# Graph layers with pre-norms on one core: the variance of an older group ahead of the tick's head on VectorE, its logarithm and exponential ahead of the tick's first activations on ScalarE

## The reference, cut

```python
h = jnp.maximum(_layernorm(x, axis=-1), 0.0)
x = x + _L0_gnn_ref(h, edge_attr_32, src, dst, ...)   # attention over the edges, segment sums
h = jnp.maximum(_layernorm(x, axis=-1), 0.0)
x = x + _L1_gnn_ref(h, src, dst, ...)                 # one linear layer, mean by degrees
h = jnp.maximum(_layernorm(x, axis=-1), 0.0)
x = x + _L2_gnn_ref(h, edge_index, ...)               # two graph convolutions, with loops
h = jnp.maximum(_layernorm(x, axis=-1), 0.0)
x = x + _L3_gnn_ref(h, edge_index, ...)               # two graph convolutions, with loops
...
def _layernorm(x, axis=-1, eps=1e-05):
    m = jnp.mean(x, axis=axis, keepdims=True)
    v = jnp.var(x, axis=axis, keepdims=True)
    return (x - m) / jnp.sqrt(v + eps)
```

## Time and profile before

| | before |
|---|---|
| median of 3 runs | 2837.82 us (2832.29 to 2838.57) |
| the profiled execution's own time | 2831.61 us |
| its span | 2829.6 us |
| TensorE busy | 1862.6 us (66%) |
| VectorE busy | 1963.3 us (69%) |
| ScalarE busy | 1101.4 us (39%) |
| GpSimd busy | 1862.3 us (66%) |

### The profile page before, as it was taken

How to read it: one execution, slowest core, us unless ns; L and a number is a source line. 1 busy time by engine, 2 the same in 40 slices (tenths; PEclk the granted TensorE clock), 3 DMA queues, 4 the chain that set the end, 5 groups by cost and what they waited for, 6 DMA issues and landing times.

```text
span 2829.6 us, 25622 instructions
## 1 busy us (share of the span) xinstructions
PE 1862.6 (66%) x6464; PEld 875.8 (31%) x6464; DVE 1963.3 (69%) x3488; ACT 1101.4 (39%) x2157; POOL 1862.3 (66%) x1775
## 2 busy tenths in 40 slices
PE   1688778761888567777588856677488868882000
PEld 0333333320344233332244423333244434431000
DVE  4777777743777658999699959999599959972000
ACT  0112121120566435444366625555366636650000
POOL 0777777765775075552677756564577757777776
PEclk7889898975899879999799979999799979995555
DMA  0222222221455434332344434444334434442000
GB/s 15 57 64 64 64 77 64 64 63 44 146 176 176 158 100 136 107 109 95 89 120 128 120 90 146 153 146 149 104 121 125 123 101 140 144 131 63 23 21 20
DMA packets 228924, 285.58 MB, mean 101 GB/s; under 512 B 85309, under 2 KB 100697, under 8 KB 228652
## 3 DMA queue, kind: packets, MB, share of 16 engines
q1 hardware_dynamic: 172332, 257.60, 28.7%
q0 software_dynamic: 56448, 26.34, 5.2%
HBM read 173.01 MB, written 136.00 MB: 109 GB/s over the span
## 4 chain that ended last, share of the span: by engine, by line
DVE 28%; PE 16%; issue 13%; POOL 11%; ACT 6%; DMA 1%; DVEq 0%; SPq 0%; ACTq 0%; POOLq 0%
POOL out_dram L1705 7%; PE bank L1004 6%; DVE mn_total L1400 5%; DVE node_h L1208 5%; POOL mn_ring L447 4%; DVE node_h L1253 2%; PE bank L1756 2%; ACT node_square L1129 2%; DVE node_x L1232 2%; DVE mn_mean L1422 2%; DVE mn_cent L1424 2%; DVE mn_h L1480 2%; PE bank L1008 2%; PE bank L1013 2%; PE bank L998 2%
## 5 line engine op out<-in xcount | busy, mean ns | idle before, releaser
L447 POOL DMA_INDIRECT mn_ring<-slot_rows,addr_i x980 | 1042.4, 1064 | 620.6 <-issue 286.1
L1004 PE MATMUL bank<-node_x,center 128*128 128x512 f32 x492 | 258.4, 640 | 101.9 <-DVE node_h L1208 97.7
L447 POOL DMA_INDIRECT fr_xin<-in_x_dram,src_i x196 | 210.2, 1073 | 125.2 <-issue 125.2
L1008 PE MATMUL bank<-node_square,mean 128*128 128x512 f32 x492 | 263.3, 618 | 35.9 <-ACT node_std L1108 35.9
L447 POOL DMA_INDIRECT found<-node_table,look_i x196 | 210.7, 1075 | 89.1 <-issue 69.1
L1013 PE MATMUL bank<-node_h,wconv 128*128 128x512 f32 x492 | 267.0, 626 | 0.0
L447 POOL DMA_INDIRECT fr_xin<-in_x_dram,dst_i x196 | 204.2, 1042 | 59.7 <-issue 59.7
L595 PE MATMUL bank<-fr_s_lo,fr_s_hi 128*128 128x392 f16 x392 | 149.2, 381 | 138.0 <-DVE fr_d_lo L714 136.7
L1705 POOL DMA_INDIRECT out_dram<-keep,scat_i x196 | 192.6, 983 | 62.4 <-issue 62.4
L1018 PE MATMUL bank<-node_act,wconv 128*128 128x512 f32 x442 | 232.3, 608 | 1.2 <-ACT node_act L1123 1.2
L1123 ACT ACTIVATE node_act<-bank,bias 128x512 f32<-128x512 f32 x246 | 167.9, 682 | 126.1 <-PE bank L1013 125.8
(11 more groups left out here) (320 smaller groups left out, 3857.2 us busy)
## 6 DMA issues: line engine op xcount, KB each, us to landing
mn_ring<-local SPq DMA_DIRECT2D x120, 256.0 KB, 4.3
node_x_in<-in_x_dram SPq DMA_DIRECT2D x98, 256.0 KB, 3.0
out_dram<-node_rows SPq DMA_DIRECT2D x98, 256.0 KB, 3.3
mn_rin<-res SPq DMA_DIRECT2D x96, 256.0 KB, 3.3
local<-node_rows SPq DMA_DIRECT2D x96, 256.0 KB, 2.5
slot_rows<-keep SPq DMA_DIRECT2D x96, 256.0 KB, 2.0
mn_fcol<-f_rows SPq DMA_DIRECT2D x192, 128.0 KB, 4.1
res<-mn_x SPq DMA_DIRECT2D x72, 256.0 KB, 2.5
```

Source lines behind the costliest of these rows:

```text
L447: return eng.indirect_dma_start(out=dest, out_offset=None, in_=table, in_offset=bass.IndirectOffsetOnAxis(ap=index, axis=0), bounds_check= ...
L1004: pe.matmul(bank[i][:, :], C["center"][:, :], src, start=True, stop=True).then_inc(s["centered"][i], 1)
L1008: pe.matmul(bank[4][:, :], C["mean"][:, :], nd.square[:, i - 1, :], start=True, stop=True) \
```

## The change

Two calls change their places. On VectorE `variance` of the older group goes ahead of the tick's `head`; on ScalarE `deviation` of the older group goes ahead of the tick's `begin`. Nothing is added or taken away, no wait is changed, and the last group of a stage and all iterations without a tick keep their order.

```diff
--- before.py
+++ after.py
@@ -1548,10 +1548,11 @@
                         finish(st, g - 1)
                     if g < n - 1:
                         gather_sum(st, g + 1)
+                    if st in NORMS and g > 0:
+                        variance(st, g - 1)
                     for t in ticks[i][:1]:
                         head(t)
                     if st in NORMS and g > 0:
-                        variance(st, g - 1)
                         normalise(st, g - 1)
                     if g == n - 1:
                         finish(st, g)
@@ -1841,10 +1842,9 @@
                 for i, (st, g) in enumerate(order):
                     if st in NORMS and g > 0:
                         squares(norm_at(st, g - 1), g - 1)
+                        deviation(norm_at(st, g - 1), g - 1)
                     for t in ticks[i][:1]:
                         begin(t)
-                    if st in NORMS and g > 0:
-                        deviation(norm_at(st, g - 1), g - 1)
                     if st != "A":
                         mix(i, st, g)
                     for t in ticks[i]:
```

## The result

| | before | after |
|---|---|---|
| median of 4 runs each, taken together | 2835.07 us (2832.29 to 2838.57) | 2851.03 us (2848.83 to 2854.07) |
| the profiled execution's own time | 2831.61 us | 2848.83 us |
| its span | 2829.6 us | 2846.9 us |
| TensorE busy | 1862.6 us (66%) | 1871.2 us (66%) |
| VectorE busy | 1963.3 us (69%) | 1971.0 us (69%) |

The account below looks back on a forecast made before the run. A chain around several engines, none full, was taken to bound each norm-stage iteration. Stage A +10.2, B +0.5 and D +10.9 made +21.6 on 2831.6: 2853, or 2859 us on the runs' median scale; range 2844 to 2878.

Parts of the forecast that it names:

- both roads to L1208: Stage A: delay through ScalarE's last exponential, or through TensorE's L1008 and L1018 to L1232; both give +0.69 us.
- the 18 iterations of the forecast: Stage A: fifteen steady periods and three like them, each 0.69 us longer, 12.4 us in all.
- The three in which ScalarE waits inside the tick: Stage A: iterations where ScalarE waits for TensorE and the early pair helps: -1.1, -0.8 and -0.4 us.
- the half of the forecast: Stages B and D: longer gaps before L1008 make the clock fall in every second iteration, none certain.
- the 0.61: Stages B and D: VectorE's 0.61 us wait before mn_h goes; B keeps 0.52 an iteration, D nothing.
- the rival in which it falls nearly every time: Stages B and D: clock falls nearly always; +36 us, 2874, or +55, 2892 at 1.97 each in D; chance 0.14.
- +0.95: Stage D: cost in us of one clock fall, L1008 and L1018 both slow; 18 x 0.5 x 0.95 = 8.6.
- D's first iteration: Stage D: variance behind a gather, the tick's activations now after it, TensorE resuming at low clock; 2.3 us.
- The rival of the held clock: Stages B and D: the clock never falls; B -5.6, D +2.3, A +10.2: +7 us, 2845; chance 0.13.
- The rule that half of all time at the lower clock is lost: Stages B and D: as a rival, half of each 6.8 us fall lost, sixteen times 3.4: +69, 2907; chance 0.03.
- the cancelling one: Stage A: unseen slack takes half of the 0.69 us while the clock holds: +1, 2838; chance 0.06.
- The rival of a faster kernel: All norm stages: mn_h's wait binds everywhere; B and D give 18.7 us, A about 0.3 x 20: 2813; chance 0.04.

Follow-up runs that it names:

- e3: The changed kernel with ScalarE's old order restored in stage A alone, so the change acts in B and D: 2846.3 us, ratio 1.0038 to before.
- e6: The kernel before with the change's ScalarE order in stage A alone, B and D as before, on a second chip: ratio 1.0006 to before.
- e2: The kernel before with only ScalarE's small logarithm and exponential moved ahead, VectorE's order as before: 2909.27 us, ratio 1.0255.
- e4: The changed kernel with matmul L1013 done three times instead of once in ticks from the 30th on, shortening TensorE's gap before L1008: 2947.29 us, ratio 1.0397 to before.
- e8: The changed kernel once more, unaltered, on a second chip where before took 3326.86 us: ratio 1.0039 to before.
- e1: The kernel before with only the variance on VectorE moved ahead, ScalarE's order as before: 2816.8 us, ratio 0.9943.
- e5: VectorE as in the changed kernel, ScalarE's small pair between the tick's rectifier and logarithm, on a second chip: ratio 0.9933 to before.
- e12: The changed kernel again, unaltered, on a third chip where before took 3374.26 us: ratio 1.0039 to before.

## Why the prediction was right, and where it was off

- **Stage A: right in mechanism and in the period, its total partly by luck.** The wait came to stand before the work of the tick: 0.75 us idle before L1827 where about 0.75 was said, the period 12.69 for a forecast of 12.66, both roads to L1208 as described. e3 and e6 show it from both sides. Of the 18 iterations of the forecast 17 cost 0.72 and the one from 736.1 cost 0.54, together 12.7 for 12.4. The three in which ScalarE waits inside the tick (from 712.6, 722.9 and 943.8) gave -2.25, -0.55 and -0.21, -3.0 for the -2.3 forecast. So the profiled stage came out at +9.74 for +10.2. The same orders cost +12.9 in e2 and e4, where the clock fell in an early iteration; the forecast had no term for that.
- **Stage B: the mechanism right, the sum by errors that cancel.** The period is 14.92 where the clock holds, 0.52 under 15.44. A fall costs back 0.52, so most long iterations are at 15.44, where 15.8 was forecast. L1008 waits 2.24, forecast 2.2, in nine of the last eleven iterations with a head, and three of these nine are long, fewer than the half of the forecast. The eleven bring -4.0 (about -0.9 by the forecast), the six heads ahead of them scatter from -1.4 to +1.5 and bring +1.6 (about -1.1 by the forecast): -2.3 for -2.0. The first iteration, which like the second has no head, costs 0.5 for 2.0, the second 0.6 for 0.5. Why the first costs so little no run shows.
- **Stage D, what is kept: right.** Nothing of the 0.61, 14.96 for 14.93, since L1208 waits 0.21 for ScalarE. L1008's wait is 2.73, forecast 2.7. e4 shows D with the clock held at 325.64 us, within 0.4 of before.
- **Stage D, how often the clock falls: right, by luck.** It was 8 of 18 for half, and nine of 18 in e3. The half was read from windows over four gaps of 2.75 us in the kernel before, in one of which the clock stood at 1.00. But that window ends at 1755.50, and the clock falls at 1756.03; a longer one from the same start shows it:

```profile
1751.60:1760.00 8.40, 2.10 (x8) 1.26 (x8) 7.32 (x11) 1.72 (x4) 4.58 (x4) 0.76 0.26 86
```

  So the clock fell behind all four of those gaps, and the rows would have spoken for the rival in which it falls nearly every time. Nor is it a matter of chance in each iteration, since seven of the eight places come back in e3 and in e8.
- **Stage D, the price of a fall: mis-sized.** The step was "L1018 ends 1.99 later at full clock ... at half clock each of the two takes up to 0.85 more", which made +0.95. It took both L1008 and L1018 as slow. In most of the eight the fall came well behind the start of L1008, in the one shown as L1008 ended, so L1018 was slow and L1008 was not or only in part, and VectorE waited only 0.31 and 0.26 for it: 0.51 in five of the eight, 0.60 in the mean. Where L1008 is slow too, the price is 0.83 and 0.86 (two of the eight) and 0.96 (e2). So the working was sound for a moment that came in two of eight. It makes 4.8 us for the 8.6 of the sum.
- **D's first iteration: mis-sized.** +2.3 was forecast, +0.2 came. The delay is there: L1008 waits 6.00 us at 1694.15. But the same iteration of before also had TensorE resume at the lower clock, on L1018 and on L1004, the latter 3.47 us long at 1688.12. Now L1004 comes late enough to run at full clock. I read this off the two timelines and ran nothing for it.
- **The sum.** +21.6 forecast, +16.0 by the medians, +17.2 by the two profiled executions. In these D's terms are 5.5 too large, B's 1.8, A's 0.5; against them stand 3.4 outside the stages, and no run shows that any of it is the change's.

The rival of the held clock had the mechanism that e4 makes by force, and is out for the change itself. The rule that half of all time at the lower clock is lost (the Trainium skill, "TensorE: Matmul & The Clock Gate", "Terms") would price the 3.41 us of the fall shown at 1.7 us, as an estimate. The trace does not agree: that iteration is 0.51 longer, and those of e2 0.96. TensorE has idle time later in the iteration, in which it can catch up; that this is the reason is argued from the timelines and was not tried by a run of its own. The rival in which it falls nearly every time is out with 8 of 18, and the cancelling one with A's 12.69 and a clock that does not hold. The rival of a faster kernel is out as well, and e1 shows why: what it wanted is to be had from VectorE's half alone, which the other half spoils. That half, the variance ahead and the pair of ScalarE left where it was, is the best version on the first chip, at 2816.8 us against 2835.1 and 2851.0; the pair between (e5) was not run there.

## What to carry to other kernels

In a queue that keeps its order, move the instruction that produces early, and leave the one that waits for it behind ready work that is as long as the wait; moved to the front together with its producer, it turns its wait into idle time for all behind it. Try the two halves of such a move apart, since here one was worth -18 us and the other +74. And where a shift lengthens TensorE's gap in each iteration, look in the trace at which instruction the lower clock would begin before pricing it: the same 3.41 us at the lower clock cost 0.51 where they began behind L1008 and 0.96 where they began with it.

## What was not expected of the hardware

- A gap of 2.73 us before L1008, the same in 15 iterations of D, was followed by the lower clock in eight of them; one of 2.24 in B in three of nine. With 1.01 in its place (e4), and with the 1.44 of before and of e1, the periods of D show no such iteration. Elsewhere shorter gaps were followed by a fall: 1.94 us in stage A in e2, 1.87 before L1004 in stage B in e1. So these runs show no length that is safe in all places.
- The long iterations of D are mostly the same ones in each execution: seven of the eight come back in e3, seven in e8 on another chip, and four in e12 on a third. In the first execution no two of them follow each other; in e3 three stand in a row. What picks them the runs do not settle.
- Two other chips ran the same kernel in 3327 and 3374 us for 2835, TensorE, VectorE and ScalarE standing idle for up to some 25 us before single instructions while GpSimd mostly went on. The cause is open.
